# Attention: tile 11's weighting ahead of the text sum, the image sums in the next step's run, and two scalings moved to steps 3 and 9

## The chip, the cores and the metric

The kernel runs on one core of a Trainium2 chip. The metric is the device time of one execution in microseconds. Engines: PE is TensorE (PEld its weight loads), DVE is VectorE, ACT is ScalarE, POOL is GpSimd, and SP issues the DMAs.

## The reference

A gated cross-attention block and a mixture-of-experts block follow each other, for 4 batches of 512 queries of width 512 and a context of 1601 rows (257 of an image, 1344 of text). The change touches the attention alone:

```
q = rms_norm(x Wq + bq);  k, v = context projections (own weights for image and text)
img_x = softmax(q k_img^T / sqrt(32)) v_img        # 16 heads of width 32
txt_x = softmax(q k_txt^T / sqrt(32)) v_txt
out   = (txt_x + img_x) Wo + bo;   x = x + tanh(g) out
```

## The kernel before, in words

The program has three stages: the projections, the attention (about 397 to 1213 us of the profiled execution), and the experts. Instructions stand in each engine's stream in a fixed order, and engines wait for each other's counters.

**Rounds and steps.** The attention has 16 rounds (G = 0 to 15), each with four heads of one batch. A round has 13 steps (kt = 0 to 12), one for each tile of 128 keys: tiles 0 to 9 are text, tile 10 is 64 rows of text and 64 of the image, tiles 11 and 12 (65 rows) are image. Each step scores its tile for four heads (`score`, L988, into three PSUM banks in turn), and ACT writes the exponentials into one of four buffers `P` (L1124).

**Units.** A softmax needs a maximum of the scores first. Beside round G's scores, TensorE computes the scores of round G+1 in 64 pieces, the *units* (L445, 448 or 258 columns, into three other banks in turn), and DVE reduces each to a maximum (L638). `UNITS` says how many stand in each step (7, 6, 4, 6, 5, 6, 6, 5, 6, 5, 6, 2, 0), and `place(i)` where: units and scores alternate. A unit's matmul waits until DVE has read the unit three before it. Round 15 has no units, since no round follows.

**Runs of narrow matmuls.** `weigh` multiplies a tile's exponentials with the values, and `total` with a block of ones, each as four matmuls of 32 columns of the array, one for each head, side by side (L943; the profile counts each as two). They stand together after a step's second unit: a *run*. While TensorE is in a run it makes no unit. Text tiles 1 to 9 are first added up in `sacc` (POOL's and DVE's additions, L1309, L1210, L1217), so that one `total` over `sacc` does for them.

**The round's end.** Bank 6 of `ps` collects the weighted values, bank 7 the sums, first for the text and then for the image. In step 11 the text's weighted values are complete (ACT copies them to `ot2`), in step 12 `both_halves_of_10` adds tile 10's text half to bank 7 and opens the image in bank 6, and DVE's last addition to `sacc` ends. In step 0 of the next round `image` does four things in one run: the total over `sacc` (which waits for that last addition and completes the text's sum), the weighting of tile 11, a wait until ACT has copied the text's sum from bank 7 to `rt2`, and then the image totals of tiles 10 and 11, which overwrite bank 7. In step 1 `image_end` weighs and sums tile 12.

**The three scalings.** With T and I the text's and the image's sums, the result is (txt I + img T) / (T I). DVE makes the three products in step 2, between units: `oi` = bank 6 times T (L1235), `ot` = txt times I (L1238), `rt` = T times I (L1241). SP sends `rt` through DRAM into a narrow tile `rc` (steps 3 and 4), DVE inverts it in step 8 (L1257), SP spreads it again in steps 9 and 11, and POOL combines all in step 12 (`normalise`).

Of the kernel before, what the change touches and what calls it, by code (L numbers as in the profile page):

```python
# [10 lines left out]
ALU = mybir.AluOpType  # L11
# [13 lines left out]
NG = 4 * NB  # L25
# [13 lines left out]
def program(nc, ap, ctx):  # L39
    pe, dve, act, pool, sp = nc.tensor, nc.vector, nc.scalar, nc.gpsimd, nc.sync  # L40
# [847 lines left out]
    def sp_attend():  # L888
        all_projected(sp)
        sp.dma_start(wo[:], ap["o_wT"].rearrange("(k p) o -> p k o", p=128)).then_inc(s_wo, 16)  # L890
        load_queries(2)
        load_values(1)
        for step in range(NSTEP):
            G, kt = divmod(step, NKT)
            pG = G - 1
            if kt == 12 and G + 1 < NG:
                store_mrow(G + 1)
            if kt == 1 and G >= 1 and pG + 2 < NG:
                sp.wait_ge(p_pv, pv_no(pG, 12))
                load_values(pG + 2)  # L900
            for i in range(3):
                if step == LASTG + 2 + 3 * i:
                    if i == 0:
                        sp.wait_ge(p_pv, pv_no(NG - 2, 12))
                        sp.wait_ge(p_sc, exp_no(NG - 2, 12, 3))
                    else:
                        sp.wait_ge(a_early, i)
                        sp.wait_ge(d_early, i)
                    for q in range(2):
                        sp.dma_start(early[:, :, 256 * q:256 * q + 256], first_weights(2 * i, q)).then_inc(s_gu, 16)  # L910
            if kt == 2 and G < NG:
                sp.dma_start(Xg[1024 * G:1024 * G + 1024, :], ap["zeros"]).then_inc(s_zero, 16)
            if 1 <= G < NG:
                rt = rt2[:, pG % 2, :]
                if kt == 3:
                    sp.wait_ge(d_img, 2 * pG + 2)
                    sp.dma_start(Td, rt[0:128:32, :]).then_inc(s_den, 16)
                if kt == 4:
                    sp.wait_ge(s_den, 112 * pG + 16)
                    sp.dma_start(rc[:], Td.rearrange("h (b c) -> (h b) c", c=16)).then_inc(s_den, 16)  # L920
                if kt == 9:
                    sp.wait_ge(d_inv, G)
                    sp.dma_start(Rd.rearrange("h (b c) -> (h b) c", c=16), rc[:]).then_inc(s_den, 16)
                if kt == 11:
                    sp.wait_ge(s_den, 112 * pG + 48)
                    for j in range(4):
                        sp.dma_start(rt[32 * j:32 * j + 32, :], Rd[j].partition_broadcast(32)).then_inc(s_den, 16)
            if kt == 5 and G + 2 < NG:
                sp.wait_ge(p_sc, exp_no(G, 4, 3))
                load_keys(G + 2, 0, last=640)  # L930
            if kt == 10 and G + 2 < NG:
                sp.wait_ge(p_sc, exp_no(G, 9, 3))
                load_keys(G + 2, 0, first=640)
            if kt == 12 and G + 2 < NG:
                sp.wait_ge(p_sc, exp_no(G, 12, 3))
                load_keys(G + 2, 1)
                if G + 3 < NG:
                    load_queries(G + 3)
# [13 lines left out]
    def pe_attend():  # L952
# [38 lines left out]
        def weigh(G, kt, p0, p1_, first, last):  # L991
            s = G % 2
            if kt == 0:
                pe.wait_ge(s_val[s], 80 * (G // 2 + 1))
                if G:
                    pe.wait_ge(d_oi, G)
                else:
                    pe.wait_ge(a_tr, NTR)
                    pe.wait_ge(d_tr, NTR)
            pe.wait_ge(a_exp, exp_no(G, kt, 3))  # L1000
            pe_heads(6, lambda j: Vg[s][p0:p1_, kt, 32 * j:32 * j + 32], P[slot(G, kt)], p0, p1_, first, last).then_inc(p_pv, 1)
# [18 lines left out]
            tot.then_inc(p_tot, 1)  # L1020
            pv.then_inc(p_pv, 1)

        def image(G):
            pe.wait_ge(d_add, 3 * G + 3)
            pe_heads(7, lambda j: ones[:, :], sacc, 0, 128, False, True).then_inc(p_tot, 1)
            weigh(G, 11, 0, 128, False, False)
            pe.wait_ge(a_txt, 2 * G + 2)
            total(G, 10, 64, 128, True, False)
            total(G, 11, 0, 128, False, False)

        def image_end(G):
            weigh(G, 12, 0, 65, False, True)
            total(G, 12, 0, 65, False, True)

        for step in range(NSTEP):
            G, kt = divmod(step, NKT)
            more = G + 1 < NG
            plan = PLAN[kt] if more else [0] * 7
            at = sum(map(sum, PLAN[:kt])) if more else 0
            upto = [at + sum(plan[:i]) for i in range(8)]  # L1040

            def place(i):
                units(G + 1, upto[i], plan[i])

            def scored(j):
                if G < NG:
                    score(G, kt, j)

            if kt == 0:
                place(0)  # L1050
                place(1)
                if G:
                    image(G - 1)
                place(2)
                for j in range(4):
                    scored(j)
                    place(3 + j)
                continue
            scored(0)
            place(0)  # L1060
            scored(1)
            place(1)
            if kt == 1 and G:
                image_end(G - 1)
            if kt == 3:
                weigh(G, 0, 0, 128, True, False)
            if 3 <= kt < 11:
                weigh(G, kt - 2, 0, 128, False, False)
            if kt == 11:
                text_end(G)  # L1070
            if kt == 12:
                both_halves_of_10(G)
                if more:
                    pe.wait_ge(d_mx, G + 2)
                    pe.wait_ge(d_ra, ra)
                    pe_mrow(BANKS_RA[(ra - 65) % 3])
                    ra += 1
            place(2)
            scored(2)
            place(3)  # L1080
            scored(3)
            place(4)
            place(5)
            place(6)
            if G in PROJECTED and kt in (4, 6, 8, 10):
                b = PROJECTED[G]
                if kt == 4:
                    pe.wait_ge(a_ath, 4 * b + 4)
                    pe.wait_ge(g_atl, 4 * b + 4)
                    if b == 0:  # L1090
                        pe.wait_ge(g_wol, 4)
                pe_project_tile(b, (kt - 4) // 2, ra_bank())
                ra += 1
# [102 lines left out]
    def dve_attend():  # L1196
# [4 lines left out]
        def units(G, m, n):  # L1201
            nonlocal ra
            for i in range(m, m + n):
                dve_max_unit(i, ra, BANKS_RA[(ra - 65) % 3])
                ra += 1
# [13 lines left out]
        for step in range(NSTEP):  # L1219
            G, kt = divmod(step, NKT)  # L1220
            pG = G - 1
# [6 lines left out]
            if kt == 2 and 1 <= G < NG:  # L1228
                units(G + 1, at, upto[2] - at)
                dve.wait_ge(p_pv, pv_no(pG, 12))  # L1230
                dve.wait_ge(a_txt, 2 * pG + 2)
                if pG:
                    dve.wait_ge(g_atl, pG)
                    dve.wait_ge(a_ath, pG)
                dve.tensor_tensor(oi[:], ps[:, 6, :], rt2[:, pG % 2, :], ALU.mult).then_inc(d_oi, 1)  # L1235
                units(G + 1, upto[2], plan[2])
                dve.wait_ge(p_tot, 5 * pG + IMAGE_TOTAL)
                dve.tensor_tensor(ot2[:, pG % 2, :], ot2[:, pG % 2, :], ps[:, 7, :], ALU.mult).then_inc(d_img, 1)  # L1238
                units(G + 1, upto[3], plan[3])
                dve.wait_ge(d_oi, G)  # L1240
                dve.tensor_tensor(rt2[:, pG % 2, :], rt2[:, pG % 2, :], ps[:, 7, :], ALU.mult).then_inc(d_img, 1)  # L1241
                units(G + 1, upto[4], sum(plan[4:]))
            elif kt == 11:
                units(G + 1, at, sum(plan))
                if more:
                    dve_text_maxima(G + 1, ra)
                add_half_of_7(G)
                add_to_sum(G, 8)
            elif kt == 12:
                add_to_sum(G, 9)  # L1250
                if more:
                    dve_rows_low(G + 1, BANKS_RA[(ra - 65) % 3])
                    ra += 1
            else:
                if kt == 8 and 1 <= G < NG:
                    dve.wait_ge(s_den, 112 * pG + 32)
                    dve.reciprocal(rc[:], rc[:]).then_inc(d_inv, 1)  # L1257
                units(G + 1, at, sum(plan))
# [911 lines left out]
```

## Time and profile before

| | |
|---|---|
| time, median of 3 runs | 1778.53 us (1777.74 to 1778.68) |
| profiled execution | 1782.02 us, its span 1780.4 us |
| busy share of the span | PE 95%, PEld 63%, DVE 67%, ACT 46%, POOL 51% |
| mean granted TensorE clock | 0.991 of full |

Matmuls are pipelined and the profile models their ends, so the 95% are no measure of how much more TensorE could do. The gap between the profiled execution's time and its span is 1.6 us.

### The profile page before, as it was taken

The numbers are of one execution on the slowest core, as the hardware profiler recorded it, in microseconds if no ns is written. First come the engines' busy times: TensorE is split into PE (matmuls) and PEld (weight loads), VectorE is DVE, ScalarE is ACT, GpSimd is POOL, SyncE is SP. The second block draws the span as 40 slices with busy tenths as digits, with TensorE's granted clock in tenths as the row PEclk, the third lists the DMA queues.
The fourth block names the chain that finished last, engine by engine and source line by source line (L and its number), as shares of the span: only waits on it lengthen the run. The fifth ranks groups of instructions, "written<-read, shape, count | busy, mean of one in ns | idle before, by whom it ended". The sixth has DMA issues, their size and how long they took to land. (4 is left out here: it accounts for less than half of the span.)

```text
span 1780.4 us, 24680 instructions
## 1 busy us (share of the span) xinstructions
PE 1697.7 (95%) x8694; PEld 1114.1 (63%) x8694; DVE 1196.7 (67%) x2229; ACT 819.6 (46%) x1519; POOL 906.3 (51%) x323
## 2 busy tenths in 40 slices
PE   5999999999999999999999999996999999999999
PEld 3888878884444444444444444443777778888777
DVE  5776677658888876888778888846445354434555
ACT  4443332336556654665556666662221255554221
POOL 3121312116766663777736667770423477776542
PEclk9999999999999999999999999998999999999999
DMA  9456858547555552555445544221211478787442
GB/s 315 141 167 190 239 177 214 183 142 193 133 133 147 146 146 48 130 146 145 121 129 141 123 107 127 74 90 41 97 70 67 158 255 270 265 269 230 154 118 95
DMA packets 198603, 273.03 MB, mean 153 GB/s; under 512 B 30969, under 2 KB 128009, under 8 KB 197965
## 3 DMA queue, kind: packets, MB, share of 16 engines
q1 hardware_dynamic: 193360, 254.67, 48.9%
q0 software_dynamic: 5120, 16.78, 2.8%
q8 instruction: 70, 1.15, 0.3%
q14 instruction: 53, 0.43, 0.1%
HBM read 198.15 MB, written 106.18 MB: 171 GB/s over the span
## 5 line engine op out<-in xcount | busy, mean ns | idle before, releaser
L1124 ACT ACTIVATE P<-ps 128x512 f32<-128x512 f32 (+1 forms) x832 | 444.4, 597 | 294.7 <-PE ps L988 257.6
L638 DVE TENSOR_REDUCE mp<-ps 128x1 f32<-128x448 f32 x768 | 429.5, 615 | 107.1 <-PE ps L445 105.4
L1309 POOL TENSOR_TENSOR sacc<-sacc,P 128x2048 f32<-128x2048 f32 x96 | 406.6, 4235 | 13.8
L445 PE MATMUL ps<-Kst,Qst 96*128 96x448 f32 (+1 forms) x1024 | 385.2, 391 | 6.4 <-DVE mp L638 6.1
L988 PE MATMUL ps<-Qst,Kst 100*128 100x512 f32 (+1 forms) x832 | 321.8, 407 | 10.7 <-ACT P L1124 10.7
L445 PEld LDWEIGHTS ps<-Kst,Qst 96*128 96x128 f32 x1024 | 192.4, 188 | 217.8 <-DVE mp L638 152.9
L943 PE MATMUL ps<-P,Vg 128*32 128x512 f32 (+2 forms) x1664 | 217.9, 605 | 0.0
L814 POOL TENSOR_TENSOR cl<-craw,ch 128x1024 fp32r<-128x1024 f32 (+2 forms) x26 | 62.3, 2398 | 287.0 <-ACT ch L550 287.0
L988 PEld LDWEIGHTS ps<-Qst,Kst 100*128 100x128 f32 (+1 forms) x832 | 152.2, 185 | 67.5 <-ACT P L1124 45.8
L49 PE MATMUL ps<-W,ch 128*128 128x512 f32 (+1 forms) x408 | 162.6, 399 | 0.0
L51 PE MATMUL ps<-W,cl 128*128 128x512 f32 (+1 forms) x408 | 159.7, 391 | 0.0
L50 PE MATMUL ps<-W,ch 128*128 128x512 f32 (+1 forms) x408 | 159.4, 391 | 0.0
L2069 POOL TENSOR_TENSOR gul<-gur,guh 128x2048 fp32r<-128x2048 f32 x15 | 69.4, 4625 | 115.1 <-ACT guh L1742 115.1
L638 DVE TENSOR_REDUCE mx<-ps 128x1 f32<-128x258 f32 x256 | 96.1, 420 | 31.6 <-PE ps L445 31.1
L1309 POOL TENSOR_TENSOR sacc<-P 128x2048 f32<-128x2048 f32 x16 | 73.3, 4582 | 61.3 <-ACT P L1124 35.6
L2069 POOL TENSOR_TENSOR Kst<-gur,Kst 128x2048 fp32r<-128x2048 f32 x15 | 69.3, 4623 | 45.7 <-ACT Kst L1742 45.7
L51 PEld LDWEIGHTS ps<-W,cl 128*128 128x128 f32 (+1 forms) x408 | 75.8, 186 | 17.8 <-issue 0.2
L1317 POOL TENSOR_TENSOR oi<-oi,ot 128x512 f32<-128x512 f32 x15 | 19.1, 1275 | 132.9 <-DVE sacc L1217 132.9
L49 PEld LDWEIGHTS ps<-W,ch 128*128 128x128 f32 (+1 forms) x408 | 76.1, 187 | 15.4
L50 PEld LDWEIGHTS ps<-W,ch 128*128 128x128 f32 (+1 forms) x408 | 76.2, 187 | 15.3
L570 ACT ACTIVATE junk<-kf 128x512 f32<-128x512 f32 (+1 forms) x51 | 32.2, 630 | 107.0 <-DVE kf L686 107.0
L943 PEld LDWEIGHTS ps<-P,Vg 128*32 128x32 f32 (+2 forms) x1664 | 36.3, 108 | 68.2 <-ACT P L1124 35.2
(240 smaller groups left out, 3078.2 us busy)
## 6 DMA issues: line engine op xcount, KB each, us to landing
gur<-in_w_gate_up SPq DMA_DIRECT2D x23, 1024.0 KB, 7.8
Kst<-KHd SPq DMA_DIRECT2D x56, 320.0 KB, 4.8
Vd<-vf SPq DMA_DIRECT2D x50, 256.0 KB, 2.3
craw<-in_ctxT SPq DMA_DIRECT2D x24, 512.0 KB, 4.6
KHd<-sth SPq DMA_DIRECT2D x24, 512.0 KB, 3.5
KLd<-stl SPq DMA_DIRECT2D x24, 512.0 KB, 4.6
dnr<-in_w_down SPq DMA_DIRECT2D x23, 512.0 KB, 3.8
xg<-Xg SPq DMA_DIRECT2D x23, 512.0 KB, 8.0
```

The source lines that it names most:

```text
L49: pe.matmul(out, ah, bh, start=first, stop=False)
L50: pe.matmul(out, ah, bl, start=False, stop=False)
L51: return pe.matmul(out, al, bh, start=False, stop=last)
L445: pe.matmul(ps[:, bank, 0:c1 - c0], Qst[G % 3][0:96, j, 128 * qt:128 * qt + 128], Kst[G % 2][0:96, j, c0:c1], start=True, stop=True).then_ ...
L570: act.activation(junk[:rows], kf[:rows, u % 3, :], ACT.Square, accum_out=stk[:rows, u % 4, 0:1]).then_inc(a_sqk, 1)
L638: dve.reduce_max(out, ps[:, bank, 0:c1 - c0], AX.X).then_inc(d_ra, 1)
L814: pool.tensor_tensor(cl[:, n % 3, :, 0:c1 - c0], craw[:, n % 3, :, 0:c1 - c0], ch[:, n % 2, :, 0:c1 - c0].bitcast(F32), ALU.subtract).then ...
L943: ins = pe.matmul(ps[32 * j:32 * j + 32, bank, :], w(j), pt[p0:p1_, j, :], start=first, stop=last, tile_position=(p0, 32 * j))
L988: pe.matmul(ps[:m, 2 + (e - 1) % 3, :], Kst[s][0:100, j, 128 * kt:128 * kt + m], Qst[G % 3][0:100, j, :], start=True, stop=True).then_inc( ...
L1124: act.activation(P[slot(G, kt)][:m, j, :], ps[:m, 2 + (e - 1) % 3, :], ACT.Exp, scale=SCALE).then_inc(a_exp, 1)
L1309: pool.tensor_tensor(sacc[:, h], (P[slot(G, 0)] if kt == 1 else sacc)[:, h], P[slot(G, kt)][:, h], ALU.add).then_inc(g_sum, 1)
L2069: pool.tensor_tensor(gul[q % 2], gur[raw_slot(q)][:], guh[q % 2].bitcast(F32), ALU.subtract).then_inc(g_gu, 1)
```

## The change

In step 0 the run now holds the weighting of tile 11 first and the total over `sacc` behind it, and nothing else. The wait for ACT's copy and the image totals of tiles 10 and 11 go to step 1, ahead of tile 12's weighting and total. Of DVE's three multiplies `oi` stays in step 2, `rt` goes to step 3 (after that step's third unit), and `ot` to step 9 (after its second unit). SP's two transfers of `rt` move one step later, and the first waits for one product where it waited for two.

```diff
@@ sp_attend
-                if kt == 3:
-                    sp.wait_ge(d_img, 2 * pG + 2)
+                if kt == 4:
+                    sp.wait_ge(d_img, 2 * pG + 1)
                     sp.dma_start(Td, rt[0:128:32, :]).then_inc(s_den, 16)
-                if kt == 4:
+                if kt == 5:
                     sp.wait_ge(s_den, 112 * pG + 16)
@@ pe_attend
-        def image(G):
+        def text_sum(G):
+            weigh(G, 11, 0, 128, False, False)
             pe.wait_ge(d_add, 3 * G + 3)
             pe_heads(7, lambda j: ones[:, :], sacc, 0, 128, False, True).then_inc(p_tot, 1)
-            weigh(G, 11, 0, 128, False, False)
+
+        def image_end(G):
             pe.wait_ge(a_txt, 2 * G + 2)
             total(G, 10, 64, 128, True, False)
             total(G, 11, 0, 128, False, False)
-
-        def image_end(G):
             weigh(G, 12, 0, 65, False, True)
             total(G, 12, 0, 65, False, True)
...
                 if G:
-                    image(G - 1)
+                    text_sum(G - 1)
@@ dve_attend, in kt == 2 and behind it
                 units(G + 1, upto[2], plan[2])
+                units(G + 1, upto[3], sum(plan[3:]))
+            elif kt == 3 and 1 <= G < NG:
+                units(G + 1, at, upto[3] - at)
+                dve.wait_ge(d_oi, G)
                 dve.wait_ge(p_tot, 5 * pG + IMAGE_TOTAL)
+                dve.tensor_tensor(rt2[:, pG % 2, :], rt2[:, pG % 2, :], ps[:, 7, :], ALU.mult).then_inc(d_img, 1)
+                units(G + 1, upto[3], sum(plan[3:]))
+            elif kt == 9 and 1 <= G < NG:
+                units(G + 1, at, upto[2] - at)
                 dve.tensor_tensor(ot2[:, pG % 2, :], ot2[:, pG % 2, :], ps[:, 7, :], ALU.mult).then_inc(d_img, 1)
-                units(G + 1, upto[3], plan[3])
-                dve.wait_ge(d_oi, G)
-                dve.tensor_tensor(rt2[:, pG % 2, :], rt2[:, pG % 2, :], ps[:, 7, :], ALU.mult).then_inc(d_img, 1)
-                units(G + 1, upto[4], sum(plan[4:]))
+                units(G + 1, upto[2], sum(plan[2:]))
```

TensorE's stream at the beginning of round 1, from the end of step 12 to the first unit behind the run of step 0, before (L988 are scores, L445 units, L943 the narrow matmuls of weightings and totals, an `x4` being the four heads of one):

```order
L450 MATMUL ps<-ident,mx 8x128 x4
L988 MATMUL ps<-Qst,Kst 65x512 x2
L445 MATMUL ps<-Kst,Qst 128x448 x2
L943 MATMUL ps<-sacc,ones 32x512 x4
L943 MATMUL ps<-P,Vg 32x512 x4
L943 MATMUL ps<-P,ones 32x512 x8
L445 MATMUL ps<-Kst,Qst 128x448
```

The same place now:

```order
L450 MATMUL ps<-ident,mx 8x128 x4
L988 MATMUL ps<-Qst,Kst 65x512 x2
L445 MATMUL ps<-Kst,Qst 128x448 x2
L943 MATMUL ps<-P,Vg 32x512 x4
L943 MATMUL ps<-sacc,ones 32x512 x4
L445 MATMUL ps<-Kst,Qst 128x448
```

The weighting of tile 11 (`P,Vg`) has changed places with the total over `sacc`, and the eight image totals (`P,ones x8`) are gone from here. They stand in step 1's run, which is now:

```order
L988 MATMUL ps<-Qst,Kst 128x512
L445 MATMUL ps<-Kst,Qst 128x448
L943 MATMUL ps<-P,ones 32x512 x8
L943 MATMUL ps<-P,Vg 32x512 x4
L943 MATMUL ps<-P,ones 32x512 x4
L445 MATMUL ps<-Kst,Qst 128x448
```

That run had two groups of four (tile 12's) and has four now; as many units and scores stand ahead of it as before.

DVE's stream from step 2 of round 1 on, before (L638 are the units' reductions, of 448 columns where `mp` is written first, of 258 where `mx` is):

```order
L1235 TENSOR_TENSOR oi<-ps,rt 128x512
L638 TENSOR_REDUCE mp<-ps 128x1
L1238 TENSOR_TENSOR ot<-ot,ps 128x512
L638 TENSOR_REDUCE mp<-ps 128x1
L1241 TENSOR_TENSOR rt<-rt,ps 128x512
L638 TENSOR_REDUCE mp<-ps 128x1 x28
L1257 RECIPROCAL rc<-rc 128x16
```

And now, up to step 10:

```order
L1235 TENSOR_TENSOR oi<-ps,rt 128x512
L638 TENSOR_REDUCE mp<-ps 128x1 x5
L1242 TENSOR_TENSOR rt<-rt,ps 128x512
L638 TENSOR_REDUCE mp<-ps 128x1 x25
L1262 RECIPROCAL rc<-rc 128x16
L638 TENSOR_REDUCE mp<-ps 128x1
L638 TENSOR_REDUCE mx<-ps 128x1
L638 TENSOR_REDUCE mp<-ps 128x1
L638 TENSOR_REDUCE mx<-ps 128x1
L638 TENSOR_REDUCE mp<-ps 128x1
L638 TENSOR_REDUCE mx<-ps 128x1 x3
L1246 TENSOR_TENSOR ot<-ot,ps 128x512
```

The two multiplies have left step 2; `rt` stands five units behind `oi`, and `ot` after the second unit of step 9.

## Rows read from the trace of the kernel before

**Rows 1.** Part 1 of the page: busy time by engine.
```profile
PE 1697.7 (95%) x8694; PEld 1114.1 (63%) x8694; DVE 1196.7 (67%) x2229; ACT 819.6 (46%) x1519; POOL 906.3 (51%) x323
```

**Rows 2.** Stretches: us, busy time by engine; one round; a slowed start of a round.
```profile
754.06:802.36 48.30, 46.97 (x280) 22.66 (x276) 40.38 (x74) 29.62 (x56) 33.76 (x11) 1.00 0.53 135
...
703.60:706.90 3.30, 3.30 (x16) 0.53 (x16) 1.52 (x3) 0.60 (x1) 2.50 (x2) 0.50 0.10 24
```

**Rows 3.** DVE in time, one round: start, us, operation [idle before <-releaser].
```profile
753.99 1.13 DVE L638 TENSOR_REDUCE mp<-ps 128x1 f32<-128x448 f32 x2
757.88 3.81 DVE L638 TENSOR_REDUCE mp<-ps 128x1 f32<-128x448 f32 x7 [2.75 <-PE ps L445]
762.91 3.28 DVE L638 TENSOR_REDUCE mp<-ps 128x1 f32<-128x448 f32 x6 [1.22 <-PE ps L445]
766.11 0.68 DVE L1235 TENSOR_TENSOR oi<-ps,rt 128x512 f32<-128x512 f32 x1
...
767.24 0.68 DVE L1238 TENSOR_TENSOR ot<-ot,ps 128x512 f32<-128x512 f32 x1
...
768.36 0.68 DVE L1241 TENSOR_TENSOR rt<-rt,ps 128x512 f32<-128x512 f32 x1
768.96 4.46 DVE L638 TENSOR_REDUCE mp<-ps 128x1 f32<-128x448 f32 x8
773.78 2.75 DVE L638 TENSOR_REDUCE mp<-ps 128x1 f32<-128x448 f32 x5 [0.36 <-PE ps L445]
...
790.59 1.97 DVE L638 TENSOR_REDUCE mx<-ps 128x1 f32<-128x258 f32 x5 [0.79 <-PE ps L445]
```

**Rows 4.** DVE, the first and the last of fourteen such waits, and the long one.
```profile
452.60 3.81 DVE L638 TENSOR_REDUCE mp<-ps 128x1 f32<-128x448 f32 x7 [2.75 <-PE ps L445]
...
709.56 3.81 DVE L638 TENSOR_REDUCE mp<-ps 128x1 f32<-128x448 f32 x7 [4.44 <-PE ps L445]
...
1109.61 3.81 DVE L638 TENSOR_REDUCE mp<-ps 128x1 f32<-128x448 f32 x7 [2.75 <-PE ps L445]
```

**Rows 5.** TensorE in time, the same round's steps 0 and 1.
```profile
752.28 0.57 PE L445 MATMUL ps<-Kst,Qst 96*128 96x448 f32 x2
753.53 1.06 PE L943 MATMUL ps<-sacc,ones 128*32 128x512 f32 x8 [0.67 <-DVE sacc L1217]
754.41 1.04 PE L943 MATMUL ps<-P,Vg 128*32 128x512 f32 x8
755.38 2.06 PE L943 MATMUL ps<-P,ones 64*32 64x512 f32 x16
757.37 0.47 PE L445 MATMUL ps<-Kst,Qst 96*128 96x448 f32 x1
...
760.17 0.45 PE L445 MATMUL ps<-Kst,Qst 96*128 96x448 f32 x1
760.55 1.06 PE L943 MATMUL ps<-P,Vg 65*32 65x512 f32 x8
761.43 1.04 PE L943 MATMUL ps<-P,ones 65*32 65x512 f32 x8
762.40 0.47 PE L445 MATMUL ps<-Kst,Qst 96*128 96x448 f32 x1
```

**Rows 6.** ACT and POOL in time, the same round: the copy of the text's sum, an addition.
```profile
754.66 0.60 ACT L1134 ACTIVATE rt<-ps 128x512 f32<-128x512 f32 x1 [1.01 <-PE ps L943]
...
764.31 4.58 POOL L1309 TENSOR_TENSOR sacc<-P 128x2048 f32<-128x2048 f32 x1 [2.17 <-ACT P L1124]
```

**Rows 7.** DVE in time, step 3 of round 0, which has no multiplies.
```profile
415.52 3.28 DVE L638 TENSOR_REDUCE mp<-ps 128x1 f32<-128x448 f32 x6 [1.28 <-PE ps L445]
```

**Rows 8.** TensorE and ACT in time: the start of round 6, the last round's end.
```profile
703.53 1.94 PE L943 MATMUL ps<-sacc,ones 128*32 128x512 f32 x8 [1.23 <-DVE sacc L1217]
...
1206.31 1.94 PE L943 MATMUL ps<-sacc,ones 128*32 128x512 f32 x8 [0.57 <-DVE sacc L1217]
...
1208.31 0.60 ACT L1134 ACTIVATE rt<-ps 128x512 f32<-128x512 f32 x1 [1.88 <-PE ps L943]
```

## The prediction

> **What bounds the kernel now.** I read the page's busy shares first, then one round by stretches, then DVE's and TensorE's own streams through that round. The page says PE 95% and DVE 67% [rows 1], which decides nothing: the stages differ, and a TensorE that is held up by a full bank still looks busy. So I take one round of the attention: 48.30 us, in which DVE works 40.38 us and TensorE is marked busy for 46.97 us [rows 2]. DVE's stream shows where the other 7.9 us lie: every idle stretch waits for TensorE's next unit (L445), and the largest two are 2.75 us in step 0 and 1.22 us in step 1 [rows 3]. The rest are pieces of 0.36 to 0.9 us, one behind each later step's run. DVE works in order, so a round's time is DVE's work plus DVE's waits, and what the change does can be read as a change of these waits. The pattern repeats: fourteen rounds (1 to 14) have the wait of step 0, thirteen of them with 2.75 us and one with 4.44 us [rows 4].
>
> Why DVE waits in step 0 is in TensorE's stream [rows 5]. Its two units are issued at 752.28; then the total over `sacc` waits for DVE's addition and begins at 753.53. Behind it stand the weighting (754.41), the totals that need ACT's copy (754.66 plus 0.60 us, [rows 6], so 755.38), and at 757.37 the next unit. DVE had its two units done at 755.06 (753.99 plus two at 0.533 us; six units take 3.20 us from 762.91 to 766.11, [rows 3]), and gets the next at 757.88, 0.51 us after TensorE began it.
>
> **The change part by part**, followed through this round.
>
> *Step 0.* The weighting of tile 11 needs only exponentials of step 11, so it can begin when the two units are through: the second at about 752.48, and 0.38 us later, as from 760.17 to 760.55, gives 752.86 [rows 5]. One group of four takes 0.88 us (753.53 to 754.41), so the total over `sacc` begins at 753.74 at the latest, and at 753.53 if the lead is shorter; I take 753.64. A run's last group needs 0.97 us until the next unit (761.43 to 762.40), which reaches DVE 0.51 us later: 755.12, where DVE is ready at 755.06. It was 757.88: 2.76 us earlier, with 2.66 and 2.82 as ends. No wait for ACT is left in this run; its copy ends at about 755.5 and is needed in step 1, two microseconds later.
>
> *Step 1.* Seven units and six scores follow with the spacing of before, because DVE, the scores and ACT all begin earlier by the same amount. Then the run has two groups more. Ahead of tile 12's they took 1.99 us together with the way out of the run (755.38 to 757.37); inside a longer run the second costs 0.88 instead, so 0.99 + 0.88 = 1.87 us (ends: twice 0.88, and 1.99). DVE's units are used up by then, so this counts in full: the wait of 1.22 us becomes about 3.1 us, and DVE goes on 2.76 - 1.87 = 0.89 us earlier than before. The exponentials of step 1 wait for the total of tile 10, whose buffer they overwrite, about 1.2 us; nothing is late by it, since TensorE's next score comes only behind the run.
>
> A rule bears on this sum. Rows: the eight matmuls of 64 rows take 0.99 us from the first to the next group, those of 65 and 128 rows 0.88 us, and the last group 0.97 us until the unit [rows 5]. The Trainium skill (TensorEngine Tiling (Array Packing), Key Properties) says that a change of tiling mode drains the engine; the trace agrees, with about 0.1 us at such a place. By it the change takes out one switch of six (the return to 128 rows and the 64-row group share what were two runs), which is the difference of 1.87 and 1.99 us; without it the saving would be 0.12 us less in each round.
>
> *Step 2 and step 3.* Two multiplies leave step 2: 0.59 and 0.60 us (767.24 to 768.96 with one unit of 0.533 between, [rows 3]). But they stood ahead of step 3's run, which has two groups, and covered it. In step 1 a run of two groups, entered with three units in hand, leaves DVE idle for 1.22 us; in round 0, which has no multiplies, step 3's run leaves 1.28 us idle [rows 3, 7]. Counted from when DVE could start (0.08 us before the profile's end of a unit) that is 1.30 us. Of that some was there already: the eight units from 768.96 took 4.46 us where 7 x 0.533 + 0.615 = 4.35 would do (0.615 us is one unit, 3.28 less 5 x 0.533), so 0.11 us. So: work out of step 2, -1.19; new wait in step 3, +1.19; `rt` behind that wait, where TensorE then fills its banks and DVE is the one that is waited for, +0.60. Sum +0.60 us (up to +0.70).
>
> *Step 9.* `ot` comes after the second unit, where DVE is idle for 0.79 us [rows 3], since TensorE makes the run there. Its 0.59 us fit into that. I cost it at nothing; without that cover it costs 0.59 us.
>
> *SP.* `rt` is ready at about 770.4 instead of 769.0 and goes out one step later; the inversion in step 8 is at 785.85, some 15 us on. The key loads of step 5 stand behind the second transfer now, and their keys are needed a round later. Nothing.
>
> *Sum for a round:* -2.76 + 1.87 + 0.60 + 0 = -0.29 us. With all ends one way -0.46 us, the other way +0.03 us, and +0.62 us if `ot` is bare as well. Fourteen rounds: -4.1 us (-6.4 to +0.4, or +8.7).
>
> *Last round and end.* Round 15 has no units, but its scores start 2.8 us earlier and give 1.87 us back: 0.9 us. After it the weighting of tile 11 again stands ahead of the total over `sacc`, where TensorE waited for only 0.57 us, and at half clock (the total's group took 1.94 us, [rows 8]): about 1.2 us later, and ACT's copy with it, which the chain to the last output projection follows. Together +0.3 us at half clock, -0.6 us at full: taken as +0.1.
>
> *The long wait.* The start of round 6 had 4.44 us where the others have 2.75 [rows 4]; the granted clock was 0.50 there, 1.2 GHz, after TensorE had waited 1.23 us for the addition [rows 2, 8]. With the weighting in that gap it should not recur: 1.7 us of this one execution.
>
> Against the profiled execution: 1782.02 - 4.1 + 0.1 - 1.7 = 1776.3 us. The runs shown have a median 3.5 us lower, so I don't suppose that they hold that slowed stretch, and take 1778.53 - 4.0, with a little rounding down for runs that do: 1774.4 us.
>
> **The rivals.**
> (B) *The waits only move.* Step 1's longer run and step 3's uncovered run take back all that step 0 gains. For it: every term but one is a shift between waits of the same two engines, and the net is a tenth of the gross. Against it: 0.67 us of TensorE's idle time in step 0 [rows 5] and 0.6 us of DVE's in step 9 do go. Half to none of the gain gives -0.14 to +0.03 us a round: 1776.5 to 1779 us.
> (C) *The multiply of step 9 is not hidden*: slower. From step 8 on the units are of 258 columns, and if TensorE there is itself held by DVE's last reduction, 0.59 us more of DVE's work delays the next units. -0.29 + 0.59 = +0.30 us a round, 1782.8 us, and up to 1787 with the other ends. Against it: DVE waits 0.79 us at that place, with TensorE's own run ahead of it. It decides if less than 0.59 us of that wait is there when `ot` comes.
> (D) *The multiplies meet POOL.* In step 9 one of POOL's additions of 4.58 us is always under way. If the multiply had to let it end, 2.3 us on average, less 0.2 us of idle time left, would be 2.1 us a round: 1808 us. Against it: the three multiplies of before lie between 766.11 and 769.04, within or across the addition from 764.31 to 768.89, and take 0.68 us each [rows 3, 6]. The Trainium skill (SBUF — State Buffer, Practical consequences) has such a lock for a DVE instruction with two SBUF inputs against a GpSimd instruction that reads SBUF; these have one input in PSUM, so by it nothing blocks, and the trace agrees.
>
> **How the numbers follow.** Forecast 0.52, B 0.36, C 0.10, D 0.02. A time within 0.2% (3.6 us) of 1778.53 can't be told from no change. The forecast's 4.1 us lies just beyond that bound, B within it, C and D above. So faster 0.52, same 0.36, slower 0.12. The forecast alone spans 1771 to 1776.5 us. For 8 in 10 I go down to 1770.5 (the good ends of all terms and a slowed stretch less) and up through B into the near part of C: 1781.
>
> **What would show it.** Right: in a round of the changed trace DVE waits at most 0.2 us behind the second unit of step 0, about 3.1 us in step 1, 1.2 to 1.3 us in step 3 before that step's third unit, and 0.2 us behind `ot` in step 9; the round takes 48.0 us; TensorE waits at most 0.1 us ahead of the total over `sacc`. Wrong: a wait in step 1 over 3.3 us, a second wait in steps 2 or 4, 0.4 us or more of new waits in steps 9 and 10 (C), a multiply longer than 0.7 us (D), or further stretches of granted clock 0.5 in the attention.

## The result: 4.5% slower, and where the time went

The changed kernel takes 1858.88 us (median of 4 runs, 1853.7 to 1863.96) where the kernel before took 1778.61 us in the same series: a ratio of 1.0453 [1.0426, 1.0479]. The forecast was 1774.4 us, faster, in a range of 1770.5 to 1781 us. It was wrong in sign, and the change measured is some twenty times the one forecast. Two executions far off the others of their kernels (2086 us of e1, at a mean granted clock of 0.75, and 9109 us of e5, at 1.00) are in the medians given below, but not in the ratios.

The profiled execution took 1860.83 us, 78.8 us more than that of before. The page's row of engines, against [rows 1]:

```profile
PE 1757.8 (95%) x8694; PEld 1150.9 (62%) x8694; DVE 1199.5 (65%) x2229; ACT 827.5 (45%) x1519; POOL 906.1 (49%) x323
```

The instruction counts are the same, and DVE has only 2.8 us more work. TensorE's busy time grew by 60 us with the same 8694 matmuls, so on average each took longer. The page's slices say why (the granted clock in tenths, 40 equal slices of the span):

```profile
PEclk9999999999899988999889998989899999999999
```

Eight slices stand below 9, seven of them in the attention. To see both parts of the loss, one takes the rounds apart. A round is measured here from the end of one row instruction of DVE (L648, explained below) to the end of the next. The stretches of rounds 1 to 3 of the changed kernel (us; busy time of PE, PEld, DVE, ACT, POOL; granted clock; DMA share; GB/s), and one stretch inside round 2:

```profile
445.87:496.20 50.33, 47.16 (x280) 22.71 (x272) 40.46 (x75) 29.26 (x55) 34.91 (x12) 1.00 0.51 130
496.20:553.44 57.24, 54.19 (x280) 26.79 (x272) 41.23 (x75) 30.19 (x56) 33.73 (x11) 0.85 0.45 114
553.44:605.26 51.82, 48.55 (x278) 23.90 (x272) 40.88 (x75) 30.01 (x56) 33.72 (x11) 0.97 0.50 126
499.50:516.50 17.00, 17.00 (x56) 9.08 (x57) 7.24 (x12) 6.38 (x11) 3.41 (x2) 0.50 0.68 182
```

Round 1 has the full clock and still takes 50.33 us, against 48.30 before [rows 2] and 48.0 forecast. That is the first part, a new wait of TensorE. Rounds 2 and 3 lose more, 6.9 and 1.5 us, with the granted clock at 0.50 (1.2 GHz) for 17.0 us in round 2 and for some 3 us in round 3. That is the second part. Six rounds are like round 2, seven like round 3, and only round 1 has the full clock throughout.

**The wait.** TensorE's stream at the beginning of round 2 answers [rows 5] (start, us, operation, number; in brackets the idle time before and what ended it; behind the dots stands step 1's run, at half clock):

```profile
494.36 0.56 PE L445 MATMUL ps<-Kst,Qst 96*128 96x448 f32 x2
494.85 1.07 PE L943 MATMUL ps<-P,Vg 128*32 128x512 f32 x8
495.73 1.04 PE L943 MATMUL ps<-sacc,ones 128*32 128x512 f32 x8
496.70 0.47 PE L445 MATMUL ps<-Kst,Qst 96*128 96x448 f32 x1
499.48 0.76 PE L988 MATMUL ps<-Qst,Kst 100*128 100x512 f32 x1 [2.31 <-DMA Qst<-mrl]
...
504.55 3.80 PE L943 MATMUL ps<-P,ones 64*32 64x512 f32 x16
508.12 1.93 PE L943 MATMUL ps<-P,Vg 65*32 65x512 f32 x8
509.82 1.93 PE L943 MATMUL ps<-P,ones 65*32 65x512 f32 x8
511.69 0.74 PE L445 MATMUL ps<-Kst,Qst 96*128 96x448 f32 x1
```

The run of step 0 is as short as forecast, and it no longer waits for the addition. But one unit further, the round's first score (L988) waits 2.31 us for a transfer, `Qst<-mrl`. The list of TensorE's waits (us in total, times, longest) has it as the first row (rounds 2 to 15; 2.16 us in round 1 are put down to the issue):

```profile
PE ps L988 <- DMA Qst<-mrl: 32.4, 14, 2.7
```

What is this transfer? The scores subtract each query's maximum by four more rows of `Qst` (rows 96 to 99; L988 has 100 rows where a unit has 96). When a round's units are done, ACT writes the high parts of the maxima to `mrh`, DVE the low parts to `mrl` (`dve_rows_low`, L648), and SP copies both into `Qst` (`store_mrow`, L327). DVE and SP in the changed kernel, at the same place:

```profile
495.53 0.67 DVE L648 TENSOR_TENSOR mrl<-ps,mrh 8x512 fp32r<-8x512 f32 x1
```

```profile
496.23 0.71 SPq L327 DMA_DIRECT2D Qst<-mrh  x1
496.98 0.64 SPq L327 DMA_DIRECT2D Qst<-mrl  x1
```

SP begins as L648 ends (496.20). The second issue is over at 497.62, and the score begins 1.86 us after it: 3.28 us from the end of L648 to the first score. The Trainium skill (DMA: Bandwidth & Descriptors, Anatomy of one DMA) says, of transfers that POOL issues, that most of a fixed cost of some 2 us is the landing and its receipt; these two come from SP, and the trace's 1.86 us behind the second issue is of that size. How much of it is the landing no run here shows.

Now SP and TensorE in the kernel before, in the round of [rows 5]:

```profile
754.09 0.70 SPq L327 DMA_DIRECT2D Qst<-mrh  x1
754.83 0.63 SPq L327 DMA_DIRECT2D Qst<-mrl  x1
```

```profile
757.68 0.39 PE L988 MATMUL ps<-Qst,Kst 100*128 100x512 f32 x1
```

L648 ended at 754.06 there. With the changed kernel's 3.28 us behind it, the rows could be used from about 757.34 (an estimate), while TensorE was still in the long run; the next unit came at 757.37. The first score followed 0.31 us later, at 757.68, and waited for nothing. So the rows were the next thing to be late, and only about 0.34 us (757.68 less 757.34) of the 2.76 us in step 0 was to be had for the scores.

### The profile page after: what moved, and what is told of

It is laid out like the page before. It is cut to its first block and busy times, and to the rows that moved or that the text cites. A ratio compares the mean times of both kernels' runs of the same rounds, so it can differ in the third digit from the quotient of the medians.

```text
span 1859.5 us, 24695 instructions
## 1 busy us (share of the span) xinstructions
PE 1757.8 (95%) x8694; PEld 1150.9 (62%) x8694; DVE 1199.5 (65%) x2229; ACT 827.5 (45%) x1519; POOL 906.1 (49%) x323
## 5 line engine op out<-in xcount | busy, mean ns | idle before, releaser
L1124 ACT ACTIVATE P<-ps 128x512 f32<-128x512 f32 (+1 forms) x832 | 450.0, 595 | 366.7 <-PE ps L988 311.0
L638 DVE TENSOR_REDUCE mp<-ps 128x1 f32<-128x448 f32 x768 | 436.2, 615 | 185.3 <-PE ps L445 184.7
L445 PE MATMUL ps<-Kst,Qst 96*128 96x448 f32 (+1 forms) x1024 | 402.0, 409 | 11.0 <-DVE mp L638 9.8
L988 PE MATMUL ps<-Qst,Kst 100*128 100x512 f32 (+1 forms) x832 | 345.9, 438 | 43.8 <-DMA Qst<-mrl 32.4
L445 PEld LDWEIGHTS ps<-Kst,Qst 96*128 96x128 f32 x1024 | 208.2, 203 | 221.9 <-DVE mp L638 142.7
L988 PEld LDWEIGHTS ps<-Qst,Kst 100*128 100x128 f32 (+1 forms) x832 | 166.7, 203 | 109.3 <-issue 56.0
L943 PE MATMUL ps<-P,Vg 128*32 128x512 f32 (+2 forms) x1664 | 224.2, 621 | 0.0
L638 DVE TENSOR_REDUCE mx<-ps 128x1 f32<-128x258 f32 x256 | 96.2, 420 | 24.4 <-PE ps L445 23.8
L943 PEld LDWEIGHTS ps<-P,Vg 128*32 128x32 f32 (+2 forms) x1664 | 37.1, 110 | 74.2 <-issue 36.1
```

Source lines behind the costliest of these rows:

```text
L445: pe.matmul(ps[:, bank, 0:c1 - c0], Qst[G % 3][0:96, j, 128 * qt:128 * qt + 128], Kst[G % 2][0:96, j, c0:c1], start=True, stop=True).then_ ...
L638: dve.reduce_max(out, ps[:, bank, 0:c1 - c0], AX.X).then_inc(d_ra, 1)
L943: ins = pe.matmul(ps[32 * j:32 * j + 32, bank, :], w(j), pt[p0:p1_, j, :], start=first, stop=last, tile_position=(p0, 32 * j))
L988: pe.matmul(ps[:m, 2 + (e - 1) % 3, :], Kst[s][0:100, j, 128 * kt:128 * kt + m], Qst[G % 3][0:100, j, :], start=True, stop=True).then_inc( ...
L1124: act.activation(P[slot(G, kt)][:m, j, :], ps[:m, 2 + (e - 1) % 3, :], ACT.Exp, scale=SCALE).then_inc(a_exp, 1)
```

## The experiments

The theory: the first score waits for the rows (1), and TensorE's idle time there brings the half clock with it. The rivals: step 1's longer run lowers the clock (2), the moved multiplies cost the time (3), or something else in the new order lowers the clock (4). For each kernel the 14 rounds 1 to 14 were summed from its profile (rounds 5 and 9 also hold a projection and are longer in all). In the third column stands a round of full clock without that projection. The kernels are called by the first two characters of their names below:

```
kernel                 14 rounds us   a round us   rounds under full clock   ratio of the times
before                    705.3          48.30            1                  1
changed                   784.3          50.33           13                  1.0453 [1.0426, 1.0479]
e4_old_rows               699.0          47.94            0                  0.9965 [0.9953, 0.9978]
e6_busy_wait              733.6          50.38            0                  1.0183 [1.0165, 1.0201]
e8_mrh_early              761.7          49.58            8                  1.0313 [1.0294, 1.0332]
e1_runs_only              746.8          49.69           12                  1.0327 [1.0309, 1.0346]
e2_scalings_only          712.3          48.88            0                  1.0047 [1.0033, 1.006]
e5_units_between          702.7          48.19            1                  0.9998 [0.9989, 1.0008]
e7_rows_early             690.9          47.40            0                  0.992  [0.9906, 0.9935]
e9_rows_early_alone       706.3          48.38            1                  1.0005 [0.9994, 1.0017]
```

**The wait taken away.** The changed kernel, with the rows sent in step 8 of the round before, when the rows of the previous heads are what the tiles hold (so the maxima that the scores subtract are other heads'; all work and sizes stay):

```diff
-    def store_mrow(G):
-        sp.wait_ge(d_ra, rows_ra(G) + 1)
+    def store_mrow(G, of=None):
+        sp.wait_ge(d_ra, rows_ra(G if of is None else of) + 1)
...
-            act.wait_ge(s_mrow[(G - 1) % 2], 32 * ((G - 1) // 2 + 1))
+            act.wait_ge(s_mrow[G % 2], 32 * (G // 2 + 1))
...
-            if kt == 12 and G + 1 < NG:
-                store_mrow(G + 1)
+            if kt == 8 and G + 1 < NG:
+                store_mrow(G + 1, G)
```

> The changed kernel, but each round's maxima rows are stored in step 8 of the round before, from the rows of the round before that (so the values of the maxima are the wrong heads', and the work is the same): the transfer is long done when step 0's first score comes. Theory 1 (the score's wait for the landing of the rows, which before lay under the run of step 0, is the whole cause, and the half clock follows from that wait): no wait of TensorE ahead of the first score, DVE waits at most 0.2 us in step 0 and about 3.1 us in step 1, half clock in at most two of the fourteen rounds, time 1774 us (1771 to 1779), as the sum without the transfer said. Theory 2 (the longer run of narrow matmuls in step 1 is what lowers the clock): half clock from step 1 on in most rounds, time above 1800 us.

Measured: 1772.48 us, ratio 0.9965 [0.9953, 0.9978], beside 1774.4 forecast for the change itself. DVE through one round of it:

```profile
749.34 0.67 DVE L648 TENSOR_TENSOR mrl<-ps,mrh 8x512 fp32r<-8x512 f32 x1
749.94 4.91 DVE L638 TENSOR_REDUCE mp<-ps 128x1 f32<-128x448 f32 x9
757.93 1.15 DVE L638 TENSOR_REDUCE mp<-ps 128x1 f32<-128x448 f32 x2 [3.07 <-PE ps L445]
```

Nine reductions follow without a gap (before, 2.75 us stood behind the second, [rows 3]), then comes step 1's wait of 3.07 us. No round is under full clock. This takes the whole loss away with the order of TensorE's and DVE's work left as it is, so (2), (3) and (4) fall as causes of it: the long run of step 1 and the moved multiplies are all here.

**The wait kept, the idle time filled.** Eleven matmuls of 96 rows into the first score's own bank, ahead of its wait for the rows; the score overwrites them:

```diff
+                if G:
+                    pe.wait_ge(a_exp, e - 3)
+                    for _ in range(11):
+                        pe.matmul(ps[:m, 2 + (e - 1) % 3, :], Kst[s][0:96, j, 0:m], Qst[G % 3][0:96, j, :], start=True, stop=True)
                 pe.wait_ge(s_mrow[s], 32 * (G // 2 + 1))
```

> The changed kernel with eleven extra matmuls (96 rows, 512 columns, about 0.21 us each) into the first score's own bank, ahead of its wait for the rows; the score overwrites them. They fill the wait with work and don't shorten it. Theory 1 (two costs: the wait itself, 32 us in fourteen rounds, and half clock that comes from TensorE's idle time in it, some 50 us): the first score starts as late as in the changed kernel, 3.2 us behind the end of DVE's reduction to the rows' low parts, and the clock stays full in the rounds: 1772.5 + 32 = 1805 us (1800 to 1811). Theory 4 (the half clock comes from something else in the changed order, such as the long run of narrow matmuls): half clock stays, above 1840 us.

Measured: 1810.61 us, ratio 1.0183 [1.0165, 1.0201]. TensorE, and the round's stretch:

```profile
763.47 0.47 PE L445 MATMUL ps<-Kst,Qst 96*128 96x448 f32 x1
763.77 2.70 PE L982 MATMUL ps<-Qst,Kst 96*128 96x512 f32 x11
766.32 0.40 PE L992 MATMUL ps<-Qst,Kst 100*128 100x512 f32 x1
```

```profile
762.29:812.67 50.38, 49.38 (x287) 24.77 (x283) 40.38 (x75) 29.76 (x57) 33.76 (x10) 1.00 0.51 130
```

The first score is as late as before the filling, the round is as long as the changed kernel's round 1 (50.33 us), and the half clock is gone from all rounds. So the half clock comes with the idle time, and neither with the late score nor with the runs. It also splits the loss of 79 us over the 14 rounds: the clock costs 784.3 - 733.6 = 51 us, and 733.6 - 705.3 = 28 us are left at full clock. These 28 are the wait's 35 us (733.6 less e4's 699.0) less the 6 us that the change gains without it (705.3 - 699.0). The eleven matmuls may hold a little of the 35 themselves: the first score begins 4.0 to 4.1 us after the start of L648, against 3.9 in the changed kernel. The Trainium skill (TensorE: Matmul & The Clock Gate, HAM oscillation) describes a TensorE that falls back to half clock when it waits for DMAs; the trace agrees in kind, with waits shorter than those of the page's example (2.3 us here).

**A shorter wait.** SP sends `mrh` as soon as ACT has written it, not after `mrl`:

```diff
     def store_mrow(G):
-        sp.wait_ge(d_ra, rows_ra(G) + 1)
         for p0, src in ((96, mrh), (98, mrl)):
+            sp.wait_ge(a_mh, G + 1) if p0 == 96 else sp.wait_ge(d_ra, rows_ra(G) + 1)
```

> The changed kernel, with the first of the two row transfers (the high parts) issued as soon as ACT has written them, ahead of DVE's low parts; the second then leaves SP 0.7 us sooner. Theory 1: the first score's wait falls from 2.3 to 1.6 us, 10 us in fourteen rounds, and the half clock with it or not, since its stretches depend on more than the wait's length: 1835 to 1850 us. If the landing of the rows were not what ends the wait: 1859 us.

Measured: 1835.47 us, ratio 1.0313 [1.0294, 1.0332]. SP and TensorE in round 1:

```profile
445.47 0.72 SPq L327 DMA_DIRECT2D Qst<-mrh  x1
446.83 0.65 SPq L327 DMA_DIRECT2D Qst<-mrl  x1
```

```profile
449.27 0.47 PE L988 MATMUL ps<-Qst,Kst 100*128 100x512 f32 x1 [1.40 <-issue]
```

One issue of 0.7 us is gone from the path, and the score still begins 1.8 us after the second issue ends. A round of full clock takes 49.58 us, 0.75 less than the changed kernel's: TensorE's wait is 0.76 us shorter in this round (1.40 against 2.16), so the wait goes one to one into the round's time. But the clock still falls in 8 of the 14 rounds.

**The runs alone.** The multiplies and SP's two transfers back in steps 2, 3 and 4, as before the change (the runs stay changed):

```diff
-                if kt == 4:
-                    sp.wait_ge(d_img, 2 * pG + 1)
+                if kt == 3:
+                    sp.wait_ge(d_img, 2 * pG + 2)
...
-            elif kt == 9 and 1 <= G < NG:
-                units(G + 1, at, upto[2] - at)
                 dve.tensor_tensor(ot2[:, pG % 2, :], ot2[:, pG % 2, :], ps[:, 7, :], ALU.mult).then_inc(d_img, 1)
-                units(G + 1, upto[2], sum(plan[2:]))
+                units(G + 1, upto[3], plan[3])
```

> The two runs of narrow matmuls are changed, the three multiplies and SP's transfers stand as before. Theory 1: the same wait for the rows, 2.2 to 2.4 us a round, and the same half clock; the 0.60 us a round of the multiplies' move is saved, so 1845 to 1856 us. Theory 3 (the multiplies' move, which changes what DVE and TensorE have in hand when step 3's run comes, opens the gaps that lower the clock): 1774 to 1780 us.

Measured: 1836.19 us, ratio 1.0327 [1.0309, 1.0346], faster than expected. The profiled execution, from which the rows come, is the fastest of the four, 1827.29 us; two others took 1835.49 and 1836.88 us. The wait for the rows is the changed kernel's (32.2 us in 14 waits), and a round of full clock takes 49.69 us, 0.64 less, the multiplies' share. But only one of the 14 rounds here has a long stretch at half clock, where the changed kernel has six; rounds 2 and 3:

```profile
498.00:554.33 56.33, 53.74 (x276) 26.75 (x272) 41.12 (x74) 30.07 (x57) 33.68 (x10) 0.85 0.45 116
554.33:604.06 49.73, 46.89 (x276) 22.74 (x272) 40.41 (x75) 29.68 (x57) 33.74 (x10) 1.00 0.52 131
```

Round 2 falls for 17 us and round 3 not at all. Equal waits are followed by no, short or long stretches of half clock; what decides between them these runs don't show.

**The scalings alone.** The image totals back in step 0, the multiplies moved as in the change:

```diff
-        def text_sum(G):
-            weigh(G, 11, 0, 128, False, False)
+        def image(G):
             pe.wait_ge(d_add, 3 * G + 3)
             pe_heads(7, lambda j: ones[:, :], sacc, 0, 128, False, True).then_inc(p_tot, 1)
-
-        def image_end(G):
+            weigh(G, 11, 0, 128, False, False)
             pe.wait_ge(a_txt, 2 * G + 2)
             total(G, 10, 64, 128, True, False)
             total(G, 11, 0, 128, False, False)
+
+        def image_end(G):
```

> The multiplies and SP's transfers are moved, the runs stand as before. Theory 1: no new wait for the rows, full clock; the multiplies cost 0.60 us in each of fourteen rounds by the sum of the prediction (1.19 us out of step 2, 1.19 us of new wait in step 3, 0.60 us of rt behind it, ot hidden in step 9): 1787 us (1783 to 1789). Theory 3: above 1830 us.

Measured: 1785.02 us, ratio 1.0047 [1.0033, 1.006], which is 8.4 us; a round takes 48.88 us, 0.58 more than before, and the clock is full. DVE in steps 2 and 3:

```profile
766.13 0.68 DVE L1235 TENSOR_TENSOR oi<-ps,rt 128x512 f32<-128x512 f32 x1
766.73 2.21 DVE L638 TENSOR_REDUCE mp<-ps 128x1 f32<-128x448 f32 x4
770.15 0.62 DVE L638 TENSOR_REDUCE mp<-ps 128x1 f32<-128x448 f32 x1 [1.22 <-PE ps L445]
770.69 0.68 DVE L1242 TENSOR_TENSOR rt<-rt,ps 128x512 f32<-128x512 f32 x1
```

The multiplies' part of the change costs what the prediction gave it (+0.60 us), and by itself this part is a loss.

**The image totals behind three units.** The idle time filled with units that are due anyway: all of them up to the fifth ahead of the image totals, then the scores; the multiplies as before the change.

```diff
                 place(2)
-                for j in range(4):
-                    scored(j)
-                    place(3 + j)
+                place(3)
+                place(4)
+                if G:
+                    image_totals(G - 1)
+                scored(0)
+                place(5)
+                scored(1)
+                place(6)
+                scored(2)
+                scored(3)
```

> Tile 11's weighting and the text's total lead step 0's run; then three units, then the image totals of tiles 10 and 11, and only then the first score, with the other two units and three scores behind it. The multiplies stand as before. Theory 1: the units and totals fill the time of the transfer, the first score waits at most 0.2 us; DVE's wait in step 0 is 1.3 to 1.5 us instead of 2.75, in step 1 1.2 us; TensorE saves the 0.4 us a round by which the first score stood behind the landing: 1773 us (1771 to 1776), full clock. Theory 2 and 3: no statement beyond full clock, since both runs hold at most two groups.

Measured: 1777.78 us, ratio 0.9998 [0.9989, 1.0008]: a miss, since a gain was expected. No score waits for the rows, but DVE waits 1.47, 0.61 and 1.58 us in steps 0 and 1, together 0.3 us less than the 2.75 and 1.22 us before:

```profile
754.75 1.16 DVE L638 TENSOR_REDUCE mp<-ps 128x1 f32<-128x448 f32 x2 [1.47 <-PE ps L445]
756.52 1.16 DVE L638 TENSOR_REDUCE mp<-ps 128x1 f32<-128x448 f32 x2 [0.61 <-PE ps L445]
759.26 3.28 DVE L638 TENSOR_REDUCE mp<-ps 128x1 f32<-128x448 f32 x6 [1.58 <-PE ps L445]
```

The second wait stands where scores follow each other with few units between them, and the trace shows what holds TensorE up there. ACT begins the step's first exponentials at 754.63, after waiting 2.81 us for the first score. The fourth and fifth scores, at 755.28 and 755.77, each begin 0.05 us after ACT's first and second exponentials end, and the next unit stands behind them (756.11): a score waits until ACT has freed its bank. How much of the missing gain comes from this no run shows.

**The rows made earlier.** The runs of the change with the multiplies as before, and the maxima's rows made and sent ahead: TensorE and ACT make them in step 11, DVE's L648 stands ahead of its last addition to `sacc`, SP sends `mrh` first as in e8, and the third unit goes ahead of step 0's run:

```diff
                 place(1)
+                place(2)
                 if G:
                     text_sum(G - 1)
-                place(2)
...
                 text_end(G)
-            if kt == 12:
-                both_halves_of_10(G)
                 if more:
...
+            if kt == 12:
+                both_halves_of_10(G)
...
             elif kt == 12:
-                add_to_sum(G, 9)
                 if more:
...
+                add_to_sum(G, 9)
```

> The changed runs with the multiplies as before the change, and the rows on their way earlier: the maxima are transposed in step 11 in place of step 12, DVE makes the low parts ahead of its last addition to sacc, the high parts leave at once, and a third unit stands ahead of step 0's run (since that addition now ends 0.6 us later). Theory 1: the first score doesn't wait for the landing, full clock, DVE waits about 0.2 us in step 0, 3.1 us in step 1 and nothing in step 3: 1768 us (1764 to 1772), faster than both. If the rows still come too late: a wait ahead of the first score and half clock.

Measured: 1764.86 us, ratio 0.992 [0.9906, 0.9935], faster than both kernels. TensorE and DVE at a round's start:

```profile
745.39 1.04 PE L943 MATMUL ps<-sacc,ones 128*32 128x512 f32 x8
746.36 0.50 PE L988 MATMUL ps<-Qst,Kst 100*128 100x512 f32 x1
```

```profile
742.42 0.67 DVE L648 TENSOR_TENSOR mrl<-ps,mrh 8x512 fp32r<-8x512 f32 x1
743.03 2.27 DVE L1217 TENSOR_TENSOR sacc<-sacc,P 128x2048 f32<-128x2048 f32 x1
745.23 1.67 DVE L638 TENSOR_REDUCE mp<-ps 128x1 f32<-128x448 f32 x3
747.11 3.28 DVE L638 TENSOR_REDUCE mp<-ps 128x1 f32<-128x448 f32 x6 [0.21 <-PE ps L445]
753.46 3.28 DVE L638 TENSOR_REDUCE mp<-ps 128x1 f32<-128x448 f32 x6 [3.08 <-PE ps L445]
```

With L648 over at 743.09, 3.27 us ahead of the score, the score follows the run without a wait. The wait of step 0 is 0.21 us, that of step 1 3.08. A round takes 47.40 us: 48.30 less the 0.89 us that steps 0 and 1 were forecast to gain. Steps 11, 12 and 0 have another order here than in the change, so agreement this close is partly luck.

**The earlier rows alone.** The same, but with the runs of before:

```diff
-        def text_sum(G):
-            weigh(G, 11, 0, 128, False, False)
+        def image(G):
             pe.wait_ge(d_add, 3 * G + 3)
...
+            weigh(G, 11, 0, 128, False, False)
```

> The same earlier rows in the kernel before, runs and multiplies as before. Theory 1: nothing was waiting for the rows there, so no gain; the last addition to sacc ends 0.6 us later and the third unit covers half of it: 1782 us (1778 to 1786). A gain of 5 us or more would say that the rows were late in the kernel before as well.

Measured: 1780.81 us, ratio 1.0005 [0.9994, 1.0017]. Before the change the rows were not late, and making them earlier gains nothing by itself; with the changed runs it is worth 1.0327 to 0.992.

## Why the prediction was wrong

The step that failed stands in *Step 1*: "Seven units and six scores follow with the spacing of before, because DVE, the scores and ACT all begin earlier by the same amount." TensorE's next unit did come 2.8 us earlier (0.50 us behind the end of L648 in round 2, where it was 3.31). The first score did not: it came 3.28 us behind the end of L648, where it was 3.62, since it then waits for its rows. The paragraph on SP asked only about `rt`'s transfers and the key loads, and left out the two of L327, which no line of the diff touches and which in the trace of before lie right beside the run that was cut. Followed step by step:

- *Step 0.* The run became shorter as forecast, and the weighting of tile 11 covers the wait for the addition (no idle time is left ahead of the total over `sacc`). The gain was taken back by the rows: DVE waits 2.2 to 2.4 us again at full clock, behind the third unit. Where the rows are in time the wait is gone (e4, with the change's own order) or 0.21 us (e7); the forecast was "at most 0.2".
- *Step 1.* Forecast about 3.1 us, measured 3.07 to 3.09 at full clock (7.19 in round 2, at half clock). The two added groups take 1.88 us in e4 (753.71 to 755.59), forecast as 1.87; without the switch that the prediction saw saved it would have been 1.99.
- *Steps 2 and 3.* Forecast +0.60 us, measured +0.58 (e2) and 0.64 (the changed kernel against e1). The wait in step 3 is 1.22 to 1.23 us.
- *Step 9.* `ot` is hidden, as costed. DVE in round 6, e6's profile, with 0.20 us of the 0.79 left behind it:

```profile
750.32 0.67 DVE L1250 TENSOR_TENSOR ot<-ot,ps 128x512 f32<-128x512 f32 x1
751.19 1.96 DVE L638 TENSOR_REDUCE mx<-ps 128x1 f32<-128x258 f32 x5 [0.20 <-PE ps L445]
```

- *Sum.* Forecast -0.29 us a round; with the rows out of the way it is -0.36 (e4, 47.94 us). The wait for the rows adds 2.39 us to that (50.33), and the clock 1.5 to 6.9 us more in 13 rounds.
- *Last round.* Forecast +0.1 us. Round 15 has the same wait; from the end of its L648 to `oi`, it takes 12.1 us (1230.17 to 1242.24) where it took 8.1 (1154.09 to 1162.17): +4.0, most of it at half clock. At full clock it takes 8.7 with the wait (e6) and 6.1 without (e4).
- *The long wait.* "It should not recur" failed for the same reason. The prediction had read that TensorE's granted clock fell to 0.50 after 1.23 us of idle time in round 6, and counted this one stretch as a gain; that a longer idle time in every round would bring it to nearly all of them was not asked, because no idle time was expected.
- *The rivals.* C and D did not happen. B was right in that a wait came in place of the one removed, but it looked for it in the waits already there.

The prediction's own list named "further stretches of granted clock 0.5 in the attention" as a sign that it was wrong, and that sign came.

What stays open: why waits of the same size are followed by half clock for 17 us in some rounds, 3 us in others and not at all in a few. It differs between executions too: e1's granted clock is 0.972 in the profiled one and 0.967 in two slower ones. Over the 14 rounds of the two profiled executions the changed kernel takes 37.5 us more than e1 (784.3 against 746.8). Nine of these are the multiplies', and most of the rest is its six long stretches against one.

## What to carry to other kernels

When a wait is to be removed, list every input of the instructions behind it and when each lands, DMAs above all, also those that no changed line touches: what lands 0.3 us ahead of its use limits the gain to about 0.3 us. A DMA that the profile never shows as a releaser may be hidden by the very work that is moved away. And an idle time of TensorE must be costed with the clock that it may take along; here that was the larger part, and filling the gap with matmuls whose result is thrown away would have been worth 2.6% of the changed kernel's time.

## What the runs showed of the hardware

- Two small transfers from SP, of 8 x 512 numbers each, cost 0.70 and 0.63 us to issue, one after the other, and about 1.8 us more until a matmul could use the data: 3.2 to 3.3 us from the end of the producing instruction, in the changed kernel, and 0.7 to 0.8 less with the first sent early (e8).
- One idle time of TensorE a round, in rounds where it is otherwise marked busy nearly throughout (47.16 of 50.33 us in round 1), brought its granted clock to 0.50 in 13 of 14 rounds when it lasted 2.2 to 2.3 us (the changed kernel), and in 8 of 14 when it lasted 1.4 to 1.6 us (e8). With the gap filled by matmuls (e6) no round fell. It stayed at 0.50 for up to 17 us in which TensorE was never marked idle.
- After shorter idle times ahead of the total over `sacc` the clock fell in some places and not in others: in the kernel before, 0.67 to 0.87 us in 13 of the rounds 1 to 14 left the clock full, and 1.23 us in round 6 did not [rows 8]; in e9, 1.05 to 1.06 us came in rounds 6, 10 and 14, and only round 10 fell.
